# First norm finished by tokens one pass ahead: modulation, gate times h and mean square on GpSimd and ScalarE, and a new split of the low parts

## The reference, cut to what matters

```
sa, ca, ga, sb, cb, gb = six vectors of 128 per row, from silu(c) @ wmod   (ga, gb: sign times max(|.|, 0.25))
h   = layernorm(x) * (1 + ca) + sa
n   = h * rsqrt(mean(h*h, over features) + 1e-6) * norm_w
q,k,v,zi,zf,o = products of n with Wq, Wk, Wv, wi, wf, Wo (+ biases; o through a sigmoid)
mLSTM over the tokens (q,k,v, gates zi,zf), written as a masked 512x512 product; its output times o, divided by a denominator
x   = x + ga * (h + that @ Wout)
h2  = layernorm(x) * (1 + cb) + sb
gate: top 2 of 8 experts by h2 @ Wr + br, softmax over the two
x   = x + gb * sum over experts of gate * (relu(h2 @ W1 + b1) @ W2 + b2)
```

## Time and profile before

| | us |
|---|---|
| median of 3 runs | 337.49 (337.04 to 339.55) |
| the profiled execution | 338.27 |
| its span | 336.4 |
| TensorE busy | 321.0 (95%) |
| VectorE busy | 278.9 (83%) |
| GpSimd busy | 171.5 (51%) |
| ScalarE busy | 165.5 (49%) |

### The profile page before, as it was taken

The page is one execution under the profiler, slowest core; times in us unless marked ns, Lnnn a source line. Parts: engine busy times, 40 slices in busy tenths (PEclk is TensorE's granted clock), DMA queues, the critical chain, the costliest instruction groups (busy, mean ns, idle before and its releaser), DMA issues.

```text
span 336.4 us, 5047 instructions
## 1 busy us (share of the span) xinstructions
PE 321.0 (95%) x1739; PEld 256.1 (76%) x1739; DVE 278.9 (83%) x799; ACT 165.5 (49%) x303; POOL 171.5 (51%) x173
## 2 busy tenths in 40 slices
PE   1999989999999999999999999999999999999996
PEld 0878955878687868887787868786888778777995
DVE  5486775999879996999699987999689969887874
ACT  1272332575454736555536545473655553346542
POOL 6630271268544883478526855478325852435440
PEclk9999998999999999999999999999999999999999
DMA  4770000600061005200160007100420016005201
GB/s 131 235 208 2 2 0 7 216 3 0 4 246 34 3 0 183 101 0 1 40 244 0 2 3 250 33 0 0 177 108 2 0 54 231 0 2 165 89 0 33
DMA packets 13455, 23.62 MB, mean 70 GB/s; under 512 B 1763, under 2 KB 8086, under 8 KB 12406
## 3 DMA queue, kind: packets, MB, share of 16 engines
q1 hardware_dynamic: 13202, 23.17, 20.8%
q10 hardware_dynamic: 164, 0.07, 0.1%
q0 software_dynamic: 64, 0.07, 0.1%
HBM read 21.07 MB, written 2.23 MB: 69 GB/s over the span
## 4 chain that ended last, share of the span: by engine, by line
PE 82%; DVE 7%; DMA 3%; POOL 3%; ACT 2%; issue 1%; SPq 1%; POOLq 0%; DVEq 0%
PE bank L1097 10%; PE bank L1123 8%; PE bank L1113 8%; PE bank L1098 8%; PE bank L1099 8%; PE bank L1114 8%; PE bank L1027 6%; PE bank L960 3%; PE bank L1012 3%; PE bank L975 2%; PE bank L1142 2%; DMA wmod_sb<-in_L_wmod_dram 2%; PE bank L1034 2%; PE bank L1134 1%; PE bank L1148 1%; PE bank L980 1%
## 5 line engine op out<-in xcount | busy, mean ns | idle before, releaser
L466 POOL TENSOR_TENSOR hg_lo<-hg,hg_hi 128x512 fp32r<-128x512 f32 x65 | 87.5, 1355 | 74.0 <-ACT hg_hi L520 74.0
L520 ACT ACTIVATE hg_hi<-hg 128x512 fp32r<-128x512 f32 x128 | 79.8, 629 | 75.9 <-DVE hg L849 74.7
L849 DVE SCALAR_TENSOR_TENSOR hg<-bank,neg_b,gate_bc 128x512 f32<-128x512 f32 x128 | 94.3, 742 | 23.2 <-DMA gate_bc<-gates_d 13.1
L1097 PE MATMUL bank<-h_hi,w_hi 128*128 128x512 f32 x128 | 58.2, 455 | 1.5 <-ACT gate_rows L561 1.5
L1113 PE MATMUL bank<-hg_hi,w_hi 128*128 128x512 f32 (+1 forms) x144 | 53.5, 372 | 0.0
L1123 PE MATMUL bank<-hg_lo,w_hi 128*128 128x512 f32 (+1 forms) x144 | 53.5, 371 | 0.0
L1114 PE MATMUL bank<-hg_hi,w_lo 128*128 128x512 f32 (+1 forms) x144 | 52.9, 367 | 0.0
L1098 PE MATMUL bank<-h_hi,w_lo 128*128 128x512 f32 x128 | 50.5, 395 | 0.0
L1099 PE MATMUL bank<-h_lo,w_hi 128*128 128x512 f32 x128 | 50.5, 395 | 0.0
L862 DVE TENSOR_TENSOR hg_lo<-hg,hg_hi 128x512 fp32r<-128x512 f32 x63 | 47.4, 753 | 1.1 <-ACT hg_hi L520 0.6
L435 POOL TENSOR_SCALAR var_eps<-mv 128x4 f32<-128x4 f32 x16 | 4.9, 305 | 71.0 <-DVE mv L596 71.0
(11 more groups left out here) (165 smaller groups left out, 552.2 us busy)
## 6 DMA issues: line engine op xcount, KB each, us to landing
gate_bc<-gates_d SPq DMA_DIRECT2D x8, 1024.0 KB, 6.9
gate_bc<-gates_d SPq DMA_DIRECT2D x8, 512.0 KB, 4.9
gate_bc<-gates_d SPq DMA_DIRECT2D x14, 256.0 KB, 3.5
out_dram<-x_all SPq DMA_DIRECT2D x7, 256.0 KB, 2.3
w_raw<-in_L_ffn_W_dram SPq DMA_DIRECT2D x1, 1024.0 KB, 9.5
x_all<-in_L_attn_x_dram SPq DMA_DIRECT2D x2, 256.0 KB, 4.3
wmod_sb<-in_L_wmod_dram SPq DMA_DIRECT2D x1, 384.0 KB, 5.2
out_dram<-x_all SPq DMA_DIRECT2D x2, 128.0 KB, 1.9
```

The costliest lines, as they stand in the source:

```text
L466: g.tensor_tensor(hg_lo[k][:, :], hg[k][:, :], hg_hi[k][:, :].bitcast(fp32), ALU.subtract).then_inc(s_lo_pool, 1)
L520: a.activation(hg_hi[k][:, :], hg[k][:, :], ACT.Copy).then_inc(s_hghi, 1)
L849: v.scalar_tensor_tensor(hg[k][:, :], up_bank[n % 4][:, :], neg_b1[:, n:n + 1], gate_bc[own % 2][:, n // NU, :], ALU.max, ALU.mult).then_i ...
L1097: t_.matmul(dst, w_hi, hx, start=True, stop=False)
```

## The change

For the rows 1 to 7 the first norm is finished by tokens, one pass ahead.

- GpSimd, after the plain norm, multiplies `xn[0]` by (1 + ca) and adds sa (both spread over all partitions, `sc_bc`, `sh_bc`), multiplies that h by ga into `xg` (the former `sq`) and adds it to x in place: `modulate`, four instructions of 128x512 at t = 14. At t = 16 `deviation` makes epsilon and root from sums of squares.
- ScalarE makes these sums (`squares`, four instructions of 128x128 with a sum output, t = 16, into `y_sb`, which is otherwise unused then) and scales h by the root (`normalise`, four of 128x128, t = 18). The transposed tile is then already the fully normalised one, and `hT` is a plain copy. `sq`, `h_ga` and their products on TensorE are gone, and so are VectorE's multiplications by the root: `zo`, `zg` are two additions each, `vs` a copy.
- v and o move from t = 9 to t = 8, and the three small steps behind them one t earlier (F at 10, its transposes and `m_row` at 11).
- `POOL_STEPS` goes from (1, 8, 9, 10, 11, 12, 13, 14, 15) to (1, 2, 3, 8, 9, 13).
- Row 0 is worked as before. In pass -2 GpSimd also makes four diagonal matrices, TensorE spreads them in two pairs of 512-column products (`spread`), and ScalarE copies the results out (`spread_copies`, `ga_copies`).

```diff
-    POOL_STEPS = (1, 8, 9, 10, 11, 12, 13, 14, 15)
+    POOL_STEPS = (1, 2, 3, 8, 9, 13)
...
+            def modulate(r):
...
+                g.tensor_tensor(h, h, spread(sc_bc), ALU.mult).then_inc(s_hs, 1)
+                pool.wait_ge(s_hs, r)
+                g.tensor_tensor(h, h, spread(sh_bc), ALU.add).then_inc(s_h, 1)
+                pool.wait_ge(s_h, r)
+                pool.wait_ge(s_gabc, 1)
+                pool.wait_ge(s_ms, 1)
+                g.tensor_tensor(xg3, h, spread(ga_bc), ALU.mult).then_inc(s_xgp, 1)
+                pool.wait_ge(s_xgp, r)
+                g.tensor_tensor(x_row, x_row, xg3, ALU.add).then_inc(s_xg, 1)
+
+            def deviation(r):
+
+                pool.wait_ge(s_msq, r)
+                g.tensor_scalar(ms_n[:, :], msq[:, :], 1.0 / D, RMS_EPS, ALU.mult, ALU.add).then_inc(s_msn, 1)
+                pool.wait_ge(s_msn, r)
+                g.tensor_tensor(rms_n[:, :], ms_n[:, :], minus_half[:, :], ALU.pow).then_inc(s_rmsn, 1)
...
+                    if ahead and t == (9 if first else 14):
+                        modulate(b + 3)
+                    if ahead and t == 16:
+                        deviation(b + 3)
...
+            def squares(r):
...
+                for j in range(NT):
+                    last = a.activation(y_sb[:, j * P:(j + 1) * P], xn[0][:, j, :], ACT.Square, accum_out=msq[:, j:j + 1])
...
+            def normalise(r):
+
+                act.wait_ge(s_rmsn, r)
+                act.wait_ge(s_xgp, r)
+                for j in range(NT):
+                    last = a.activation(xn[0][:, j, :], xn[0][:, j, :], ACT.Copy, scale=rms_n[:, j:j + 1])
+                last.then_inc(s_hn, 1)
...
-                    if t == 6 and start:
+                            a.activation(hT[:, :], bA[:, :], ACT.Copy).then_inc(s_hT, 1)
+                    if t == 6 and first:
...
-                    if t == 8 and start:
+                    if t == 8 and first:
...
+                    if ahead and t == 16:
+                        squares(b + 3)
+                    if ahead and t == 18:
+                        normalise(b + 3)
...
+                        if t == 8 and m2 > 0:
+
+                            dve.wait_ge(s_vz, m2 + 1)
+                            for h in range(2):
+                                last = v.tensor_tensor(zo[:, 2 * h:2 * h + 2, :], vz[h][:, :, NZ:NVO],
+                                                       bo_bc[:, :].unsqueeze(1).to_broadcast([P, 2, DH]), ALU.add)
+                            last.then_inc(s_zo, 1)
...
-                        for j in range(NT):
+                        for j in range(NT if m1 == 0 else 0):
                             t_.matmul(bC[:, j * P:(j + 1) * P], h_ga[:, j * P:(j + 1) * P], ident[:, :], start=j == 0, stop=False,
...
-                    if t == 7:
+                    if t == 7 and m2 == 0:
 
                         pe.wait_ge(s_sq, m2 + 1)
...
-                    if t == 9 and start:
+                    if t == (9 if first else 8) and start:
...
+                    if first and t in (7, 16):
+                        spread(0 if t == 7 else 1)
```

More of the change, by code:

```diff
@@ L451, in body @@
                         norm(1, m1)
-                    if t == 8 and start:
+                    if first and t == 10:
+                        diagonals(1)
+                    if t == 8 and first:
                         pool.wait_ge(s_mse, m2 + 1)
@@ L547, in body @@
                                      scale=mods[:, 4, bass.ds(m1, 1)]).then_inc(s_h2, 1)
-                    if t == 10 and start:
+                    if t == (10 if first else 9) and start:
                         act.wait_ge(s_zo, m2 + 1)
@@ L964, in chain @@
                     if t == 4:
[L965 removed]
+                        if m2 == 0:
+                            pe.wait_ge(s_xn[0], 1)
+                        else:
+                            pe.wait_ge(s_hn, m2)
                         if end:
@@ L1028, in chain, with spread, keep_busy @@
                         last.then_inc(s_pv, 1)
-            def keep_busy(n):
+            def spread(n):
+                pe.wait_ge(s_dg, n + 1)
+                if n:
+                    pe.wait_ge(s_sbc, n)
+                for k in range(2):
+                    last = t_.matmul(bank[2 + k][:, :], ones[:, :], diag(n, k), start=True, stop=True)
+                last.then_inc(s_spr, 1)
+            def keep_busy(n, dst):
                 for _ in range(n):
-                    t_.matmul(bank[3][:, 0:P], ident[:, :], ones[:, :], start=True, stop=True)
+                    t_.matmul(dst[:, 0:P], ident[:, :], ones[:, :], start=True, stop=True)
             def keep_busy_wide(n):
@@ L1068, in body @@
                         first_gates(B - 1)
+                    if first and t == LAG + 1:
+                        pe.wait_ge(s_dve0, 1)
+                    if opening and t == LAG + 1:
+                        pe.wait_ge(s_sbc, 2)
                     if first and t > LAG or opening and LAG < t < 8:
-                        keep_busy(2)
+                        keep_busy(2, bank[4] if first else bank[3])
                     if opening and t == 8:
```

109 lines of the change are left out of this document (92 added, 17 removed).

## The result

| | before | after |
|---|---|---|
| median of 4 runs on one chip, us | 337.26 | 360.88 (355.49 to 362.23) |
| the profiled execution, us | 338.27 | 360.33 |
| its span, us | 336.4 | 358.6 |
| granted clock of TensorE | 0.995 | 0.962 |

The changed kernel takes 1.062 times as long (95% interval 1.056 to 1.069). It was forecast slower, at 354 us with a range of 337 to 365. The direction and the mechanism held; the size was 7 us short.

The account below looks back on a forecast made before the run. A loop through VectorE's gates, transfer, `hg`, `ew` and `y_sb` was to replace TensorE as bound: 13.0 (passes 0 to 4) + 1.1 (pass 5) - 0.4 (pass 6) + 3.0 (opening) = 16.7 us, giving 354 us (337 to 365).

Parts of the forecast that it names:

- The second loop: VectorE's work up to the gates, transfer, `hg`, `ew`, product, `y_sb`, next pass: nearly as long as TensorE's own loop.
- rival 3: TensorE stays the bound, gates' transposes starting within 1.5 us of step 14's last product; 332.7 us, chance 0.14.
- The gates held by GpSimd: GpSimd's four instructions at t = 14 hold VectorE's small products, so the gates end 1.3 us later per pass.
- three casts: Nearest rows for VectorE's holding by GpSimd: first waits 1.08, second slips through, third waits 0.98 us.
- `hg_lo` of step 15 and the scalings: End of pass: VectorE's `hg_lo` before the `ew` costs 0.6 us, ScalarE's four scalings ahead of `y_sb` cost 0.7.
- Pass 5 and the passes 6 and 7: Pass 5, without `modulate` and scalings, was put at +1.1 us; pass 6 at -0.4.
- The opening: Passes -2 and -1, where spreading products delay TensorE's queue: +3.0 us for both (0 to 5).
- a gift: Pass -1 gives a part back: logits were taken at 50.07 though TensorE had them 2 us before.
- Less holding (345 us): Rival 1: at the gates, small products slip between GpSimd's instructions; a pass costs 1.0 us, 345 us, chance 0.17.
- the balance (336 to 340): Rival 4: stalls of 1 to 1.5 us per pass eat TensorE's 1.23; 336 to 340 us, chance 0.12.
- The strict lock (365 us): Rival 2: all four small VectorE products at the gates wait for GpSimd; 4.7 us per pass, 365 us, chance 0.11.
- the two terms of the tail: End of pass: 0.6 us for VectorE's `hg_lo` of step 15 and 0.7 for ScalarE's scalings ahead of `y_sb`.

Follow-up runs that it names:

- b1_split: Kernel before with only `POOL_STEPS` changed, to (1, 2, 3, 8, 9, 13); 350.40 us, 1.0404 of the kernel before.
- b4_less_pe: Kernel before, rows 1 to 7 without TensorE's `h_ga` transposes and with one sum-of-squares product in place of four; 347.36 us, 1.0257 of the kernel before.
- e2_fill: Changed kernel with three filler products on TensorE ahead of its wait for the gates; 360.41 us, 1.0681 of the kernel before.
- e3_tail: Changed kernel with the `hg_lo` of step 15 back on GpSimd and the scalings behind the `y_sb` copy; 352.01 us, 1.0377 of the kernel before.
- e1_mod_waits: Changed kernel with GpSimd waiting for the gates before its four `modulate` instructions; 353.24 us, 1.0484 of the kernel before.
- e4_all: Changed kernel: `modulate` behind the gates, `hg_lo` of step 13 on VectorE, of 15 on GpSimd, scalings behind `y_sb`; 338.38 us, 1.0065 of the kernel before.

## Why the prediction was right, and where its sizes were off

- **The second loop as the bound of the changed kernel: right.** TensorE idles ahead of the gates' transposes, for 17.4 us in all, and the chain goes through VectorE. The test given for rival 3 fails: the transposes start 2.2 to 3.4 us behind the last product. That this loop was as long as TensorE's own in the kernel before is borne out by `b1_split`. `b4_less_pe` agrees that TensorE's microsecond, taken alone, gives nothing back, but the place is another one: TensorE does not wait at the gates there, it waits for `vs` at t = 10.
- **The gates held by GpSimd, 1.3 us: right in kind, too small.** Ahead of the gates VectorE did wait for the logits, 0.74 against my 0.6. `top_g` and one more held, as I had counted, is what pass 3 shows: the gates end 27.96 us after the start of the pass against 26.76, 1.2 later. But in the passes 0, 1, 2 and 4 all three were held, some 2.3 later in the passes 1, 2 and 4. This was the step that failed: I read from three casts that every second small instruction slips through, and let one of `gate_a`, `gate_b`, `gates` wait. The one that always slips is that right behind the held `top_g`, so it is `gate_a`; `gate_b` is held in every full pass, and `gates` in four of the five. The four are not fixed: in `e2_fill`, whose GpSimd and VectorE have the same instructions, it is none of five. GpSimd's instructions also took 1.28 each and not 1.04.
- **`hg_lo` of step 15 and the scalings, 0.6 + 0.7: right as a sum.** At full clock the rows give 1.3. The medians of `e3_tail` say the same, but in part by luck, as told above. The slack ahead of the `y_sb` transposes, which I took as 0.6 from the chain of waits, is 0.44 by TensorE's timeline, where they start at 208.71 and not at 208.87.
- **The missing term: TensorE's clock.** From the gates to the next pass it took 11.9, 11.9, 11.2 and 11.0 us in the passes 1 to 4 instead of 9.7 in the mean: 1.8 more, of which 1.3 was in the sum. Most of the other 0.5 goes with the long low stretches of the passes 1 and 2, by the comparison with `e2_fill`; the medians showed no gain there.
- **Pass 5 and the passes 6 and 7: right** within 0.4 each. In pass 5 `gate_b` and `gates` are not held, in line with there being no `modulate`.
- **The opening: right in its number, in part by luck.** The sum of both passes was 2.7 against 3.0. But the logits of row 0 were taken at 52.41, later than the 50.07 of the earlier trace rows; this part I had called a gift, and it was none. The transposes of the first gates start only 0.9 us later than before (55.71 against 54.82). The other 1.8 come behind them, where TensorE runs 3.4 us at its lower clock from 59 us on; the kernel before had its full clock there. The sum had no term for that.
- **The rivals.** Less holding (345 us) and the balance (336 to 340) fell with the held products. The strict lock (365 us) is nearer in time than its picture was: not all four wait.

Divided up by the rows, a pass of the passes 1 to 4 is longer by 2.0 us at the gates (the mean of 2.3, 2.3, 1.2 and 2.4) and by 1.8 behind them, of which 1.3 are the two terms of the tail. That is 3.8 where the prediction had 2.6. The five full passes came out 6.4 us above its 13.0, and its other terms together 0.9 below.

## What to carry to other kernels

Before work is moved to an idle engine, look at what the busy one does in those very microseconds: a GpSimd instruction that reads SBUF stretched a VectorE product of 32 numbers per partition (`gate_b`) from 0.19 to 1.24 us, and the same GpSimd work begun behind the gates (`e1_mod_waits`, `e4_all`) did not. And before work is taken off TensorE, look at where it would have to wait instead: if another loop is as long as its own, the saving becomes a gap, and behind a gap of one microsecond the lower clock can cost more than was saved. When two kernels differ by a few microseconds, count also how often such a near thing fell either way in each.
